# A second scan state whose drive TensorE makes from a diagonal matrix

## The reference

```
dA  = exp(dt * A)                  # decay, per channel, state and time
dBu = dt * B[time, state] * u      # drive
h   = dA * h + dBu                 # the scan
y   = sum over states of h * C[time, state]
```

## Time and profile before

| | us |
|---|---|
| time, median of 3 runs | 2102.48 |
| the profiled execution's own time | 2102.38 |
| its span | 2100.6 |
| PE busy | 1995.7 |
| PE weight loads busy | 1549.1 |
| VectorE busy | 1472.6 |
| GpSimd busy | 1438.2 |
| ScalarE busy | 1202.7 |

### The profile page before, as it was taken

One profiled execution on the slowest core, in us unless ns is written; L12 is line 12 of the kernel. 1 busy time (PEld: TensorE's weight loads), 2 busy tenths in 40 slices (PEclk: granted clock), 3 DMA queues, 4 the chain that ended last, 5 costly groups with the idle time before them and its releaser, 6 DMA issues. The chain is left out here.

```text
span 2100.6 us, 42996 instructions
## 1 busy us (share of the span) xinstructions
PE 1995.7 (95%) x14582; PEld 1549.1 (74%) x14583; DVE 1472.6 (70%) x2715; ACT 1202.7 (57%) x2403; POOL 1438.2 (68%) x973
## 2 busy tenths in 40 slices
PE   7998999999999989999999999999799999999998
PEld 5886447999999746666666666666564499999994
DVE  6887684333333489999999999999976733333335
ACT  5675523222222269999999999999853232222222
POOL 6775004777777439999999999999940067777660
PEclk9999999999999999999999999999999999999999
DMA  8000100000000433333333333333342000000004
GB/s 312 1 0 2 41 1 16 25 25 25 26 24 25 105 105 106 99 107 108 106 109 112 102 106 103 107 107 103 91 188 101 3 25 25 25 25 25 24 24 124
DMA packets 83096, 146.44 MB, mean 70 GB/s; under 512 B 18555, under 2 KB 52349, under 8 KB 80806
## 3 DMA queue, kind: packets, MB, share of 16 engines
q1 hardware_dynamic: 73894, 126.36, 18.9%
q0 software_dynamic: 9088, 18.63, 3.2%
HBM read 128.04 MB, written 16.94 MB: 69 GB/s over the span
## 5 line engine op out<-in xcount | busy, mean ns | idle before, releaser
L2406 POOL TENSOR_TENSOR m_seen<-m_state,experts 128x1024 f32<-128x1024 f32 (+1 forms) x256 | 598.9, 2370 | 19.1 <-DVE m_state L2461 13.5
L2461 DVE TENSOR_TENSOR_SCAN m_state<-experts,ps 128x512 f32<-128x512 f32 x448 | 537.1, 1232 | 2.2 <-issue 1.5
L2197 ACT ACTIVATE experts<-delta,experts 128x512 f32<-128x512 f32 x448 | 291.3, 713 | 0.3
L1933 PE MATMUL ps<-ident,m_seen 128*128 128x128 f32 x2040 | 269.4, 276 | 21.0 <-POOL m_seen L2406 20.7
L1933 PEld LDWEIGHTS ps<-ident,m_seen 128*128 128x128 f32 x2040 | 236.4, 142 | 57.2 <-POOL m_seen L2406 37.5
L1596 POOL COPY f_weights<-experts 128x1898 f32 x142 | 252.0, 1775 | 23.9 <-issue 23.5
L1419 PE MATMUL first_up_ps<-f_xT,f_weights 128*128 128x128 f32 x1988 | 241.4, 275 | 1.7 <-issue 1.7
L1419 PE MATMUL ps<-zu,f_weights 128*128 128x128 f32 x1988 | 241.4, 275 | 1.7 <-issue 1.7
L1419 PEld LDWEIGHTS first_up_ps<-f_xT,f_weights 128*128 128x128 f32 x1988 | 233.2, 192 | 2.5 <-issue 2.5
L1419 PEld LDWEIGHTS ps<-zu,f_weights 128*128 128x128 f32 x1988 | 233.2, 192 | 2.5 <-issue 2.5
L2441 DVE TENSOR_TENSOR ps<-m_delta_u,ps 128x512 f32<-128x512 f32 x256 | 172.1, 672 | 4.0 <-PE ps L1877 4.0
(11 more groups left out here) (473 smaller groups left out, 3913.9 us busy)
## 6 DMA issues: line engine op xcount, KB each, us to landing
experts<-m_rows SPq DMA_DIRECT2D x144, 512.0 KB, 3.7
experts<-in_experts SPq DMA_DIRECT2D x17, 1461.0 KB, 18.0
tokens<-f_rows SPq DMA_DIRECT2D x8, 512.0 KB, 5.8
f_rows<-expert_out SPq DMA_DIRECT2D x8, 512.0 KB, 7.3
f_cols<-expert_out SPq DMA_DIRECT2D x8, 512.0 KB, 7.2
experts<-m_diagonal SPq DMA_DIRECT2D x16, 256.0 KB, 4.2
out<-X SPq DMA_DIRECT2D x4, 512.0 KB, 3.2
X<-in_x SPq DMA_DIRECT2D x4, 448.0 KB, 5.8
```

What stands on the lines that cost most here:

```text
L1933: mm = pe.matmul(Y[:, i // 2, at:at + P], seen[:, n % SEEN, h, i * P:(i + 1) * P], ident[:], is_transpose=True, start=(n == 0 and at == 0) ...
L2197: act.activation(PB[n % B_RING][:, h, :] if n in AWAY else dA[:, n % DECAYS, h, :], delta[:, U % 2, h, :], ACT.Exp, scale=decay[:, lhn:lhn ...
L2406: pool.tensor_tensor(seen[:, n % SEEN, :, part], state[:, n % RING, :, part], row.unsqueeze(1).to_broadcast([P, HALF, row.shape[-1]]), ALU ...
L2461: dve.tensor_tensor_scan(state[:, n % RING, h, :], decay_, drive_, before_, ALU.mult, ALU.add).then_inc(s_state, 1)
```

## The change

The set DIAGONAL holds states 7 and 11 where it held 11 alone. State 7's drive is no longer made by VectorE from B spread in PSUM, but by `cross` on TensorE, straight into PB, as state 11's. This needs a second matrix of 128x512 in SBUF. It stands in a new tile, counting, in which five constants of the feed-forward layer's router stand too (all_ones, before, lane, tile_number, ones_tile; they had tiles of their own). Since the scan stage overwrites them, SyncE loads them again at the start of the second feed-forward layer, ahead of the eight experts' weights, and two places there wait for it. In the scan stage SyncE writes zeros to two DRAM arrays, and for each unit writes two diagonals and loads two matrices (state 7's into the old place, state 11's into counting).

```diff
--- before
+++ after
@@ tiles at the start of the kernel
-        ones_tile = sb("ones_tile", [P, NT])
-        all_ones = sb("all_ones", [P, P])
-        before = sb("before", [P, P])
+        counting = sb("counting", [P, SEG])
+        all_ones, before, lane = (counting[:, k * P:(k + 1) * P] for k in range(3))
+        tile_number, ones_tile = counting[:, 3 * P:3 * P + SLOTS], counting[:, 3 * P + SLOTS:3 * P + SLOTS + NT]
         ahead = sb("ahead", [P, E])
-        tile_number = sb("tile_number", [P, SLOTS])
         tile_start = sb("tile_start", [P, SLOTS])
-        lane = sb("lane", [P, P])
...
+        again = [x for x in shapes if x[1] in ("ones_tile", "all_ones", "before", "tile_number", "lane")]
+        COUNTING_IN = lambda n: EXPERTS_IN + 16 * len(again) * n
@@ router counts, VectorE and TensorE
                                 dve.wait_ge(s_count, 1)
+                                dve.wait_ge(experts_in, COUNTING_IN(n))
...
                                     pe.wait_ge(s_taken, 1)
+                                    pe.wait_ge(experts_in, COUNTING_IN(n))
@@ SyncE, second feed-forward
                             if n:
+                                for dst, name in again:
+                                    sp.dma_start(dst[:], a[name]).then_inc(experts_in, 16)
                                 for e in range(E - LODGERS, E):
                                     load_expert(sp, e, lodgers_in)
@@ scan stage
-                DIAGONAL = 11
+                DIAGONAL = (7, 11)
...
-                diagonal = lodge(SEG)
+                diagonal = [lodge(SEG), counting[:]]
...
-                diagonal_out = nc.dram_tensor("m_diagonal", (P * (SEG + 1),), F32, kind="Internal").ap()
+                diagonal_out = [nc.dram_tensor(f"m_diagonal_{k}", (P * (SEG + 1),), F32, kind="Internal").ap() for k in range(len(DIAGONAL))]
...
-                nth_upright = {G: k for k, G in enumerate(G for G in range(STEPS) if G in nth_across or G % NS == DIAGONAL)}
+                nth_upright = {G: k for k, G in enumerate(G for G in range(STEPS) if G in nth_across or G % NS in DIAGONAL)}
@@ SyncE, scan stage
-                        sp.dma_start(whole_out, diagonal).then_inc(s_rows_out, 16)
-                        sp.wait_ge(s_rows_out, 16)
+                        for k in range(len(DIAGONAL)):
+                            sp.dma_start(whole_out[k], diagonal[0]).then_inc(s_rows_out, 16)
+                        sp.wait_ge(s_rows_out, 16 * len(DIAGONAL))
...
-                            wait(sp, s_diagonal, 16 * V)
-                            sp.dma_start(entries_out, rows_out[V % 2][DIAGONAL, :].rearrange("(i p) -> p i", p=P), allow_slow_non_contiguous=True).then_inc(s_rows_out, 16)
+                            wait(sp, s_diagonal, 16 * V * len(DIAGONAL))
+                            for k, n in enumerate(DIAGONAL):
+                                sp.dma_start(entries_out[k], rows_out[V % 2][n, :].rearrange("(i p) -> p i", p=P), allow_slow_non_contiguous=True).then_inc(s_rows_out, 16)
...
-                                        sp.wait_ge(s_upright, (nth_upright[(V - 1) * NS + DIAGONAL] + 1) * HALF)
-                                    sp.dma_start(diagonal, whole_out).then_inc(s_diagonal, 16)
+                                        sp.wait_ge(s_upright, (nth_upright[(V - 1) * NS + DIAGONAL[-1]] + 1) * HALF)
+                                    for k in range(len(DIAGONAL)):
+                                        sp.dma_start(diagonal[k], whole_out[k]).then_inc(s_diagonal, 16)
@@ TensorE, scan stage
-                            pe.wait_ge(s_diagonal, 16 * (U + 1))
+                            pe.wait_ge(s_diagonal, 16 * (U + 1) * len(DIAGONAL))
...
-                                mm = pe.matmul(PB[n % B_RING][:, h, i * P:(i + 1) * P], across[:, i, h * P:(h + 1) * P], diagonal[:, i * P:(i + 1) * P], start=True, stop=True)
+                                mm = pe.matmul(PB[n % B_RING][:, h, i * P:(i + 1) * P], across[:, i, h * P:(h + 1) * P], diagonal[DIAGONAL.index(n)][:, i * P:(i + 1) * P], start=True, stop=True)
...
-                            if G % NS == DIAGONAL:
+                            if G % NS in DIAGONAL:
                                 cross(G, h)
```

More of the change, by code:

```diff
@@ L1665, in mamba @@
                 scaled = lodge(SCALED * TILES * DI).rearrange("p (r i d) -> p r i d", r=SCALED, d=DI)
-                diagonal = lodge(SEG)
+                diagonal = [lodge(SEG), counting[:]]
                 assert room[0] <= LODGERS * EXPERT
-                diagonal_out = nc.dram_tensor("m_diagonal", (P * (SEG + 1),), F32, kind="Internal").ap()
-                whole_out = diagonal_out[0:P * SEG].rearrange("(p t) -> p t", t=SEG)
-                entries_out = diagonal_out.rearrange("(p f) -> p f", f=SEG + 1)[:, 0:SEG:P]
+                diagonal_out = [nc.dram_tensor(f"m_diagonal_{k}", (P * (SEG + 1),), F32, kind="Internal").ap() for k in range(len(DIAGONAL))]
+                whole_out = [x[0:P * SEG].rearrange("(p t) -> p t", t=SEG) for x in diagonal_out]
+                entries_out = [x.rearrange("(p f) -> p f", f=SEG + 1)[:, 0:SEG:P] for x in diagonal_out]
                 rows_out = [nc.dram_tensor(f"m_rows_{k}", (2 * NS, SEG), F32, kind="Internal").ap() for k in range(2)]
@@ L1719, in stored @@
                 def stored(V):
-                    return 16 * (2 + V * 2)
+                    return 16 * (len(DIAGONAL) + V * (1 + len(DIAGONAL)) + 1)
                 PAIR_OF = [slice(j * SEG // 2, (j + 1) * SEG // 2) for j in range(2)]
@@ L1794, in _ @@
                             sp.dma_start(b_rep, rows_out[V % 2][AWAY[0]:NS:AWAY[1] - AWAY[0], :].unsqueeze(0).to_broadcast([P, len(AWAY), SEG])).then_inc(s_b_rep, 16)
-                            wait(sp, s_diagonal, 16 * V)
-                            sp.dma_start(entries_out, rows_out[V % 2][DIAGONAL, :].rearrange("(i p) -> p i", p=P), allow_slow_non_contiguous=True).then_inc(s_rows_out, 16)
+                            wait(sp, s_diagonal, 16 * V * len(DIAGONAL))
+                            for k, n in enumerate(DIAGONAL):
+                                sp.dma_start(entries_out[k], rows_out[V % 2][n, :].rearrange("(i p) -> p i", p=P), allow_slow_non_contiguous=True).then_inc(s_rows_out, 16)
                             for g in range(GROUPS):
                                 if g == DIAGONAL_BEFORE:
-                                    sp.wait_ge(s_rows_out, stored(V) + 16)
+                                    sp.wait_ge(s_rows_out, stored(V) + 16 * len(DIAGONAL))
                                     if V:
-                                        sp.wait_ge(s_upright, (nth_upright[(V - 1) * NS + DIAGONAL] + 1) * HALF)
-                                    sp.dma_start(diagonal, whole_out).then_inc(s_diagonal, 16)
+                                        sp.wait_ge(s_upright, (nth_upright[(V - 1) * NS + DIAGONAL[-1]] + 1) * HALF)
+                                    for k in range(len(DIAGONAL)):
+                                        sp.dma_start(diagonal[k], whole_out[k]).then_inc(s_diagonal, 16)
                                 Q = V * GROUPS + g
@@ L2158, in round_high @@
                             act.activation(bc[0:XR], SIDE1[0:XR], ACT.Copy).then_inc(s_bc, 1)
-                            wait(act, s_b, ((V - 1) * (NS - len(AWAY) - len(ACROSS) - 1) + 1) * HALF if V > 1 else 0)
+                            wait(act, s_b, ((V - 1) * (NS - len(AWAY) - len(ACROSS) - len(DIAGONAL)) + 1) * HALF if V > 1 else 0)
                             act.activation(parts[0:32, V % 2, :], SIDE1[0:32], ACT.Copy).then_inc(s_rounded, 1)
@@ L2206, in delta_u_across @@
                             if V:
-                                act.wait_ge(s_upright, (nth_upright[(V - 1) * NS + DIAGONAL] + 1) * HALF)
+                                act.wait_ge(s_upright, (nth_upright[(V - 1) * NS + DIAGONAL[-1]] + 1) * HALF)
                             for k, (s_side, s_read, nth) in enumerate(((s_side0, s_read0, nth0), (s_side1, s_read1, nth1))):
@@ L2376, in _ @@
                     def _(pool):
-                        pool.memset(diagonal, 0.0)
+                        pool.memset(diagonal[0], 0.0)
                         pool.memset(hT[:, :, 0:PAD], 0.0).then_inc(s_hT, 1)
```

## The result

The changed kernel takes 2116.38 us (median of 6 runs, 2112.14 to 2119.49), the kernel before 2102.15 us beside it (2100.67 to 2104.64, 6 runs): ratio 1.0060, 95% interval 1.0048 to 1.0071. It is slower, by 14.2 us in the medians.

A forecast was written before the change was run, and what follows sets the result against it. VectorE was taken to set the scan stage's pace, the other engines close behind; TensorE's added 1.33 us a unit, less what VectorE gains, summed over units to +10.2 us on 2102.38, giving 2112.6 us, range 2101 to 2121.

The forecast's parts named there:

- the sum: Scan stage: gains and losses added over the 16 units by kind, +10.2 us, giving 2112.6 us.
- A cross: TensorE, between output projection and next unit's projection: two halves add 1.33 us a unit, delaying all it does there.
- What VectorE gives up: State 7's two drives: 1.16 us a unit, 18.6 us in 16 units if nothing else holds VectorE.
- the wait at the drive of state 9: VectorE waits for TensorE's B matmul; closing units net +0.50 us after an upper unit, -0.24 after a lower one.
- The keep: ScalarE's copy of states 6 and 7, without slack before state 10's scan: +1.33 us in units 6, 8, 11, 13.
- GpSimd's softplus sum: Sum after ScalarE's logarithm, 0.34 us slack: 0.99 us later in opening units, passed on in units 1 to 5.
- Transfers at nothing: Second zeros, diagonal and matrix loads: 0 taken, up to 4.2 us at the start; later loads have room.
- the reload: Router constants loaded again ahead of the experts' weights: hidden by GpSimd's idle time, 0; 2.5 us if that failed.
- Units 0 and 15: First and last units: 0; unit 0 has GpSimd and ScalarE late, unit 15's wait behind GpSimd swallows the gain.
- The clock: TensorE's falls to the lower clock between units: no change taken, with ends of -0.5 and +8 us for the range.
- Rival 1: VectorE's time counts: each unit loses 1.16 us until GpSimd stops it, about -14 us, 2088.5; chance 0.11, whole or in part.

The follow-up runs named there:

- TensorE's work alone: Kernel before, with state 7's B matmul issued four times per half instead of once, VectorE's drives kept: 2114.39 us, ratio 1.0044.
- TensorE's work at state 13: Kernel before, with state 13's B matmul issued four times per half instead of once, VectorE's products kept: 2102.98 us, ratio 0.9995.
- `KEPT_FIRST = 8`: Changed kernel, with ScalarE's copy of the last columns of states 6 and 7 moved ahead of its state 8 work: 2113.01 us, ratio 1.0040.

## Why the prediction was right, and where it was not

The direction, the size (+11.7 us in the stage where the sum said +10.2) and the cause, TensorE's time ahead of L1855, held. The roads by which it reaches VectorE were named in part only. By kinds of unit, in us:

| units | predicted | changed kernel | TensorE's work alone |
|---|---|---|---|
| 1, 3, 5 | +3.0 | +3.8 | +3.7 |
| 2, 4 | +0.9 | +1.2 | +1.1 |
| 6, 8, 11, 13 | +5.3 | +5.5 | +5.1 |
| 10, 12, 14 | +1.5 | +2.4 | +1.6 |
| 7, 9 | -0.5 | -0.9 | +0.1 |
| 0, 15 | 0 | -0.2 | +1.0 |

- **A cross costs TensorE 1.33 us more a unit, and that passes to L1855.** Shown: ScalarE waits 1.93 us for it in unit 13 where it had waited 0.58, +1.35.
- **What VectorE gives up is worth nothing in opening units.** Shown twice: without the products they gain 0.26 us in eight units, and with TensorE's work alone they cost what the change costs (+9.8 and +10.0).
- **Closing units, the wait at the drive of state 9.** Right in place and size: units 12 and 14 +0.58 where +0.50 stood, and the wait in unit 12 is 1.66 us, as in the sum. Units 7 and 9 are at -0.35 behind that drive where -0.24 stood. The rest of their row is the clock: unit 7 is 0.65 shorter since the fall ahead of it in the kernel before didn't come, unit 9 0.40 longer at its very end, where the next fall came. Unit 10's +1.24 isn't a mis-sized term: 0.67 of it comes at its first state, behind a fall of TensorE's clock to a mean of 0.59 of full speed, a mixture of its levels of 1.2 and 2.4 GHz, after waits of 0.91 and 1.02 us for GpSimd. With TensorE's work alone it is +0.53.

```profile
1264.00:1268.00 4.00, 3.24 (x11) 2.57 (x12) 3.70 (x6) 3.92 (x9) 4.00 (x3) 0.59 0.12 45
```
```profile
1264.76 1.97 PE L1940 MATMUL ps<-ident,m_seen 128*128 128x128 f32 x8 [1.02 <-POOL m_seen L2413]
1266.52 0.63 PE L1884 MATMUL ps<-m_parts,m_spread 96*128 96x512 bf16 x1
```

- **The keep bounds opening units.** Right as the cause and in its price (+1.36 and +1.35 in units 11 and 13 for 1.33), wrong in its first place. I looked at the keep of states 6 and 7 alone and put 1.16 us of wait at the drive of state 9. VectorE stops earlier, at the scan of state 8, for the keep of 4 and 5, which stands behind ScalarE's rounding; that wait, 1.54 us, is as new as the other. The reading of rows ended one keep too late, and it hid that two edits of ScalarE's order would be needed to undo the cost.
- **Units 1, 3 and 5, 0.99 predicted, 1.23 to 1.34 measured.** The step that failed is to let these units follow GpSimd's softplus sum. That sum did come 0.97 to 1.07 us later, as the slack of 0.34 said, but two other roads are longer: the keeps give +1.2 to +1.3 already at state 10, and with them moved ScalarE's normalised input gives the same at state 15. Both carry ScalarE's row whole, without slack. The keep's 1.33 was in the sum for units 6 to 13 and would have stood here too. Nor do the closing ones follow that sum: unit 4 pays at the drive of state 9 (a wait of 1.66 us) and ends at +0.66, unit 2 is 0.34 early behind that drive and +0.51 by state 15, at the same drive as unit 3. Their +1.2 for +0.9 is thus a near hit by another road.
- **Transfers at nothing, and as much for the reload.** Shown by the run with them alone.
- **Units 0 and 15**, where 0 stood, are +0.64 and -0.87, and neither is the cross's. The run with TensorE's work at state 13 has unit 0 at +0.64 too, late at the same states, and the changed kernel with its keeps moved has it at +0.07 and -0.04. Over all runs unit 0 goes from -0.15 to +1.03, and the low clock at the stage's start lies at another place in most. In unit 15 the transposes ahead of the second drive of state 9 took 1.97 us before, in a stretch of low clock, and 1.12 after; with `KEPT_FIRST = 8` the changed kernel has 1.97 there again, and 0.00 for the unit. Before, then after:

```profile
1522.32 1.97 PE L1933 MATMUL ps<-ident,m_seen 128*128 128x128 f32 x8 [3.44 <-POOL m_seen L2406]
```
```profile
1540.31 1.12 PE L1940 MATMUL ps<-ident,m_seen 128*128 128x128 f32 x8 [3.29 <-POOL m_seen L2413]
```

- **The clock**, taken as no change, has one fall ahead of a unit from 1 to 14 before and one in the changed kernel, at another unit. No change of their number is shown. What went with the falls and the low clock in units 10, 9, 0, 7 and 15 (+0.67, +0.40, +0.64, -0.65 and -0.87) nearly cancels, so that the total came close to the sum is in part luck.
- **Rival 1** (VectorE's time is what counts) is false at state 7, but true for closing units when TensorE is left alone: -0.76 us in units 10, 12 and 14, and the whole 1.19 us in unit 9. By the Trainium skill, "Perfetto Trace Analysis", section on identifying the most-contended engine, the engine of highest occupancy is the one to relieve; the runs agree in closing units, and disagree in opening ones (0.26 us gained in eight): there TensorE's late projection holds VectorE through ScalarE's order.

The change's idea was thus sound and its state wrong: at state 7 the cross stands between the output projection and the next unit's projection, for which ScalarE and, through the keep, VectorE wait. At state 13 the same work costs nothing in the unit where it stands. VectorE's gain is kept from unit 6 on; what units 2 and 4 gain, units 3 and 5 give back. The stage is 4.6 to 7.0 us shorter than before, the time 0.3 to 0.4% less.

## What to carry to other kernels

When work moves to another engine, look not at that engine's share but at what it has to deliver next after the place where the work goes, and who waits for that: here the same 1.3 us cost 1.3 us at one state and 0.01 at another. Before counting a gain on a busy engine, follow every buffer that it overwrites to its last reader, and that reader's own row back to what it waits for, to the first such wait and not only to the tightest; and when one road is cleared, look for the next that starts at the same late instruction. Two one-sided runs (the added work alone, the removed work alone) settle what the sum of both can't.

## What the runs showed of the hardware that was not expected

TensorE's clock falls ahead of one or two of the units 1 to 14 in seven of the 14 profiles, and of none in the other seven. The place changes: 1107 us before, 1265 in the changed kernel, 1211 with TensorE's work alone, 1404 with one keep moved, 1306 and 1353 with TensorE's work at state 13. Each fall stands some 3 us ahead of a unit's start, behind or at the end of two waits of TensorE for GpSimd of 0.7 to 1.0 us each, and costs the unit after it 0.6 to 0.9 us. The same two waits stand ahead of each of the units 7 to 14 in the kernel before, where one of them brought a fall; what picks the unit stays open. With a stage of 771.8 us, differences of 1 us between two profiles are thus no evidence unless they are spread over units of a kind.

The clock column of a window is no proof of full speed near the start of a trace: from 18 to 24 us it reads 1.00 while the matmuls of L650 take the 1.16 us of the low level.

Moving 256 KB more a unit showed nowhere: the DMA share of the stage is 0.38 against 0.34, and the transfers alone gave a ratio of 0.9994, with 1 inside its interval.
